# Perceiver block, fp32, one core: expert steps begun with the last feed-forward block, last expert units cut by token tile, and two reorderings in layer 1

## The reference, cut to what matters

```python
# layer 0 feed-forward: dense part plus experts chosen by product keys
mlp = silu(h @ Wg + bg) * (h @ Wu + bu) @ Wd + bd          # hidden width 2048
idx, scores = top-8 of the 64 sums of two top-8 key lists  # for each of 4 heads
w = silu(einsum('btd,bthkd->bthk', h, down_embed[idx])) * softmax(scores)
experts = einsum('bthk,bthkd->btd', w, up_embed[idx])      # 2048 experts
# layer 1 cross attention: 257 context rows of each sequence are memory keys and values
mem = ctx @ Wm; k = concat(xn @ Wk, mem); v = concat(xn @ Wv, mem)
# layer 1 MLP, both weights rounded to -1, 0, 1 times a scale of each row
tern = clip(round(w / scale), -1, 1); r = relu(x @ (tern_fc * s).T + low_rank); y = (r*r) @ (tern_proj * s).T
```

## Time and profile before

| what | us |
|---|---|
| median of 3 runs | 2406.06 (2401.96 to 2407.88) |
| the profiled execution's own time | 2407.21 |
| its span | 2405.4 |
| PE matmul busy | 2177.9 (91%) |
| DVE busy | 1260.4 (52%) |
| ACT busy | 897.4 (37%) |
| POOL busy | 92.1 (4%) |

### The profile page before, as it was taken

The page is one execution under the profiler, slowest core; times in us unless marked ns, Lnnn a source line. Parts: engine busy times, 40 slices in busy tenths (PEclk is TensorE's granted clock), DMA queues, the critical chain, the costliest instruction groups (busy, mean ns, idle before and its releaser), DMA issues. The chain is left out here.

```text
span 2405.4 us, 35121 instructions
## 1 busy us (share of the span) xinstructions
PE 2177.9 (91%) x14614; PEld 1527.3 (63%) x14614; DVE 1260.4 (52%) x2059; ACT 897.4 (37%) x2189; POOL 92.1 (4%) x113
## 2 busy tenths in 40 slices
PE   6988888779999999988998899999999999988889
PEld 4344344448876888743443688777877878764577
DVE  2103677745343877879998411244444353537553
ACT  1013333214333333369998223233232232323333
POOL 0000000000000000100000000000000000000022
PEclk9999988889999999989999889999999999999899
DMA  6010000002210011110002114421212121232000
GB/s 222 0 60 18 0 1 1 2 35 71 70 28 31 25 47 53 53 70 18 18 1 70 53 53 157 140 80 50 71 41 80 41 80 41 63 112 80 1 1 36
DMA packets 86482, 124.81 MB, mean 52 GB/s; under 512 B 7010, under 2 KB 48482, under 8 KB 86244
## 3 DMA queue, kind: packets, MB, share of 16 engines
q1 hardware_dynamic: 86324, 122.56, 15.7%
HBM read 107.60 MB, written 14.94 MB: 51 GB/s over the span
## 5 line engine op out<-in xcount | busy, mean ns | idle before, releaser
L1098 ACT ACTIVATE R<-bank 128x512 f32<-128x512 f32 (+1 forms) x155 | 91.8, 598 | 514.6 <-PE bank L808 336.6
L1339 ACT ACTIVATE R<-R 128x64 f32<-128x64 f32 x1024 | 248.8, 384 | 13.1 <-DVE R L1872 13.1
L808 PE MATMUL bank<-cth,wmh 128*128 128x512 f32 x512 | 209.2, 409 | 11.5 <-ACT arena L1403 5.5
L808 PE MATMUL bank<-cth,wml 128*128 128x512 f32 x512 | 203.3, 397 | 0.0
L808 PE MATMUL bank<-ctl,wmh 128*128 128x512 f32 x512 | 203.1, 397 | 0.0
L478 PE MATMUL bank<-H,arena 128*128 128x512 f32 x320 | 146.5, 612 | 1.5 <-ACT H L1159 0.8
L478 PE MATMUL bank<-XN,arena 128*128 128x512 f32 x320 | 146.8, 613 | 0.4 <-ACT R L1239 0.4
L478 PE MATMUL bank<-Y,arena 128*128 128x512 f32 x256 | 119.4, 613 | 6.1 <-ACT H L1345 6.1
L808 PEld LDWEIGHTS bank<-cth,wmh 128*128 128x128 f32 x512 | 96.9, 189 | 40.7 <-issue 21.2
L808 PEld LDWEIGHTS bank<-cth,wml 128*128 128x128 f32 x512 | 96.8, 189 | 22.4
L1976 DVE COPY Y<-bank 128x512 f32<-128x512 f32 x128 | 79.4, 683 | 59.4 <-PE bank L836 59.3
(11 more groups left out here) (377 smaller groups left out, 4314.4 us busy)
## 6 DMA issues: line engine op xcount, KB each, us to landing
H<-in_ctxT SPq DMA_DIRECT2D x30, 512.0 KB, 5.2
arena<-in_L_attn_mlp_w SPq DMA_DIRECT2D x8, 1024.0 KB, 5.4
arena<-spill SPq DMA_DIRECT2D x32, 256.0 KB, 5.6
spill<-R SPq DMA_DIRECT2D x3, 2048.0 KB, 8.3
spill<-XN SPq DMA_DIRECT2D x3, 2048.0 KB, 8.3
arena<-in_L_ffn_Wg SPq DMA_DIRECT2D x4, 1024.0 KB, 7.0
arena<-in_L_ffn_Wu SPq DMA_DIRECT2D x4, 1024.0 KB, 5.2
arena<-in_L_ffn_Wd SPq DMA_DIRECT2D x4, 1024.0 KB, 5.4
```

The lines of the kernel that those rows point to most:

```text
L808: last = mm(b[:, :].rearrange("p (a c) -> p a c", a=2), w_, c_[:, k, :, :], start=(k == 0 and n_ == 0), stop=(k == 3 and n_ == 2))
L1098: fn(dst, src, ACT.Copy).then_inc(act_bank_free, 1)
L1339: last = fn(EE[:, n % 2, a:a + 64], RC["Ey"][:, t, h, :], ACT.Copy, scale=RC["Ex"][:, t, h, 8 * j + x:8 * j + x + 1])
```

## The change: what it does

In the expert phase: ACT's first product is placed inside the last dense block, and waits for the routing of its own tile alone; a third product buffer is added (the space of `RC["s"]`), so that ACT may be three steps ahead of DVE's multiplication. DVE's routing pieces of tile 7 come one addition earlier, and its first `spread` comes before the last two additions of the dense part. POOL's sum waits for the last `hid_low` and is cut into eight instructions. The last four `cf` units are one token tile by 512 outputs each (16 matmuls of 128 columns) rather than one output group by 512 tokens, and the lag of PE and DVE shrinks over the last three steps. In layer 1: the memory units and feature transposes are interleaved, and key row 256 is computed as 24 matmuls with the 32 last context rows stationary and 512 columns of `Wm` moving (two units `mrow`), and turned by eight transposes within the first projection group. The `vT` split moves forward; block 4 is rounded in the last stage; blocks 4 and 5 are rounded between the additions of j = 0, blocks 6 and 7 between those of j = 1; the units `rs` 2 and 3 are computed between `f_down(j, 0)` and `f_down(j, 1)`.

```diff
+        EE = [RC["sim"][:, 0:4].rearrange("p t n -> p (t n)"), RC["sim"][:, 4:8].rearrange("p t n -> p (t n)"),
+              RC["s"].rearrange("p t n -> p (t n)")]
...
# PE, expert phase
-            for n in range(-LEAD, STEPS + LAG):
...
+            def factors_out(n):
...
+                if n >= STEPS - 4:
+                    for o in range(4):
+                        last = linear(b[:, tl(o)], W(("cf", j)), tl(o), SJ[j % 3], tl(t))
+                    last.then_inc(dve_bank_full, 1)
+                else:
                     linear(b[:, :], W(("cf", j)), tl(t % 4), SJ[j % 3], ch(t // 4)).then_inc(dve_bank_full, 1)
...
+            for n in range(LEAD):
+                factors_in(n)
+            for n in range(STEPS):
+                if n + LEAD < STEPS:
+                    factors_in(n + LEAD)
+                else:
+                    factors_out(2 * n - STEPS - 2)
+                factor_rows(n)
+                if n + LEAD >= STEPS:
+                    factors_out(2 * n - STEPS - 1)
+                elif n >= LAG:
+                    factors_out(n - LAG)
+            factors_out(STEPS - 2)
+            factors_out(STEPS - 1)
# PE, start of the cross attention
-            memory(0, range(2, 8))
-            for c in range(C2):
-                features(3, c)
+            memory(0, range(2, 5))
+            features(3, 0)
+            memory(0, range(5, 7))
+            features(3, 1)
+            memory(0, range(7, 8))
             pe.wait_ge(S["d_llo"], 1)
-            b = open_act("m256")
-            for o in range(OT1):
+            for h in range(2):
+                b = open_act(("mrow", h))
                 for k in range(4):
-                    wh, wl = wmh[:, o // 4, k, tl(o % 4)], wml[:, o // 4, k, tl(o % 4)]
-                    for i, (w_, c_) in enumerate(((wh, last_high), (wh, last_low), (wl, last_high))):
-                        last = mm(b[:, 32 * o:32 * o + 32], w_, c_[:, k, :], start=(k == 0 and i == 0), stop=(k == 3 and i == 2))
+                    for i, (c_, w_) in enumerate(((last_high, wmh), (last_low, wmh), (last_high, wml))):
+                        last = mm(b[0:32, :], c_[:, k, :], w_[:, h, k, :], start=(k == 0 and i == 0), stop=(k == 3 and i == 2))
...
# PE, last stage
-            scale_row(2, 8)
-            scale_row(3, 12)
...
                 f_down(j, 0)
+                if j < 2:
+                    scale_row(j + 2, 8 + 4 * j)
                 f_down(j, 1)
# ACT
+            def products(n):
+                j, t = n // TT, n % TT
+                if n < TT:
+                    act.wait_ge(S["c_fac"], n + 1)
+                if n >= 3:
+                    act.wait_ge(S["c_mul"], n - 2)
...
+                if j == NQ - 1:
+                    products(0)
                 exponentials_of(2 * j + 1)
...
-            act.wait_ge(S["c_fac"], TT)
-            for n in range(2):
-                products(n)
+            products(1)
+            act.wait_ge(S["h_low"], 32 + 8 * NQ)
+            products(2)
             act.wait_ge(dve_bank_full, UV.at[("cd", 3, C2 - 1, 3)] + 1)
-            hidden(0, 0)
-            products(2)
-            for t in range(1, 4):
+            for t in range(4):
                 hidden(0, t)
             products(3)
...
             f_up(0, 0)
+            f_up(0, 1)
+            ternary(4)
+            f_up(1, 0)
             ternary(5)
-            f_up(0, 1)
+            f_up(1, 1)
             ternary(6)
-            f_up(1, 0)
             ternary(7)
-            f_up(1, 1)
# DVE
+            LAST_PIECES = {(0, 0): 1, (0, 1): 2, (0, 2): 3, (0, 3): 4, (1, 0): 5}
...
+                        if (j, c, o) == (NQ - 1, 1, 1):
+                            spread(0, 0)
...
-            rounded(4, proj_row)
-            dve.wait_ge(S["f_vhi"], 1)
...
+            for j in range(NQ):
                 f_low(j, 0)
                 f_low(j, 1)
                 f_add(j, 0)
+                if j == 0:
+                    rounded(4, proj_row)
+                    rounded_up(5, 2)
+                elif j == 1:
+                    rounded_up(6, 3)
+                    rounded(7, proj_row)
                 f_add(j, 1)
# POOL
+            pool.wait_ge(S["h_low"], 32 + 8 * NQ)
             for c in range(C2):
-                g.tensor_tensor(Y[:, :, ch(c)], y_high[:, :, ch(c)].bitcast(f32), y_low[:, :, ch(c)].bitcast(f32), ALU.add
-                                ).then_inc(S["c_y"], 1)
+                for k in range(4):
+                    g.tensor_tensor(Y[:, k, ch(c)], y_high[:, k, ch(c)].bitcast(f32), y_low[:, k, ch(c)].bitcast(f32), ALU.add
+                                    ).then_inc(S["c_y"], 1)
```

More of the change, by code:

```diff
@@ new lines, in factors_in, with factor_rows @@
+            def factors_in(n):
+                j, t = n // TT, n % TT
+                if t == 0:
+                    weight(("ce", j))
+                b = open_act(("ce", j, t))
+                linear(b[:, :], W(("ce", j)), tl(t % 4), Y, ch(t // 4)).then_inc(act_bank_full, 1)
+                if t == TT - 1:
+                    free_after_act(("ce", j))
+            def factor_rows(n):
+                j, t = n // TT, n % TT
+                pe.wait_ge(S["c_p"], n + 1)
+                b = open_dve(("pt", j, t))
+                for e in range(4):
+                    last = nc.tensor.transpose(b[:, tl(e)], RC["pj"][:, t % 2, tl(e)], tab("ident"))
+                last.then_inc(dve_bank_full, 1)
@@ L810, in memory, with last_memory @@
                     last.then_inc(dve_bank_full if o in (2, 3) else act_bank_full, 1)
+            def last_memory():
+                on_act(("mrow", 1))
+                b = open_act("m256")
+                for o in range(OT1):
+                    last = nc.tensor.transpose(b[:, 32 * o:32 * o + 32], last_rows[0:32, tl(o)], tab("ident", 32)[:, 0:32])
+                last.then_inc(act_bank_full, 1)
             def projections():
@@ L1296, in _ @@
                 copy_out(RC["sim"][:, t, :], unit(("sim", t))[:, :])
+            def products(n):
+                j, t = n // TT, n % TT
+                if n < TT:
+                    act.wait_ge(S["c_fac"], n + 1)
+                if n >= 3:
+                    act.wait_ge(S["c_mul"], n - 2)
+                for h in range(PH):
+                    for x in range(8):
+                        a = 512 * h + 64 * x
+                        last = fn(EE[n % 3][:, a:a + 64], RC["Ey"][:, t, h, :], ACT.Copy,
+                                  scale=RC["Ex"][:, t, h, 8 * j + x:8 * j + x + 1])
+                last.then_inc(S["c_ee"], 1)
             def exponentials_of(t):
@@ L1329, in _ @@
                     split_high(piece_no[(("cd", j), o)] + PIECES)
-            def products(n):
-                j, t = n // TT, n % TT
-                if n >= 2:
-                    act.wait_ge(S["c_mul"], n - 1)
-                for h in range(PH):
-                    for x in range(8):
-                        a = 512 * h + 64 * x
-                        last = fn(EE[:, n % 2, a:a + 64], RC["Ey"][:, t, h, :], ACT.Copy,
-                                  scale=RC["Ex"][:, t, h, 8 * j + x:8 * j + x + 1])
-                last.then_inc(S["c_ee"], 1)
             def hidden(j, t):
@@ L1417, in _ @@
                 d_piece_high(n)
-            memory(0, (0, 1, 4, 5, 6, 7))
-            for c in range(C2):
+            memory(0, (0, 1, 4))
+            for c, more in ((0, (5, 6)), (1, (7,))):
                 features(3, c)
@@ L1422, in _ @@
                 fn(dx_high[:, :, ch(c)], XN[:, :, ch(c)], ACT.Copy).then_inc(S["d_xhi"], 1)
-            copy_out(RDm["m256"], unit("m256")[:, 0:256].rearrange("p (o b) -> p o b", o=8))
+                memory(0, more)
+            for h in range(2):
+                copy_out(last_rows[0:32, ch(h)], unit(("mrow", h))[0:32, :])
             for g_, (w, half) in enumerate(GROUPS):
@@ L1484, in _ @@
             fn(RE["z"][:, 0, :], RE["z"][:, 1, :], ACT.Exp).then_inc(S["e_exp"], 1)
-            for n in range(2, 5):
-                ternary(n)
             act.wait_ge(in_small, 112)
             fn(v_parts[:, 0], vT, ACT.Copy).then_inc(S["f_vhi"], 1)
+            for n in range(2, 4):
+                ternary(n)
             end_stage()
@@ new lines, in _ @@
+            for n in range(1, STEPS + 1):
+                if n < STEPS:
+                    spread(n // TT, n % TT)
+                if n + LEAD > STEPS:
+                    from_factors(2 * n - STEPS - 4)
+                weigh((n - 1) // TT, (n - 1) % TT)
+                if n + LEAD > STEPS:
+                    from_factors(2 * n - STEPS - 3)
+                elif n > LAG:
+                    from_factors(n - 1 - LAG)
+            dve.wait_ge(S["d_lhi"], 1)
+            v.tensor_tensor(last_low[:, :, :], last_raw, last_high[:, :, :].bitcast(f32), ALU.subtract).then_inc(S["d_llo"], 1)
@@ L2160, in _ @@
             low_rank()
-            f_low(0, 0)
-            rounded_up(5, 2)
-            f_low(0, 1)
```

(6 more changed lines are left out.)

133 lines of the change are left out of this document (64 added, 69 removed).

## The result

The changed kernel took 2338.5 us (median of 4 runs, 2331.7 to 2341.4) against 2405.9 for the kernel before (4 runs, 2402.0 to 2407.9). The ratio is 0.9719, 95% interval 0.9701 to 0.9737. The forecast was 2341, inside a range of 2332 to 2358. The profiled run took 2340.6 (span 2338.8), 66.6 less than the profiled run before; the four parts were to give 65.5.

The account below looks back on a forecast made before the run. PE was taken as the bound outside the expert phase, ACT as its pace inside. Terms of -20.7, -11.0, -17.5 and -16.3 sum to -65.5, from 2407.2 to 2341.7, given as 2341 us; range 2332 to 2358.

Parts of the forecast that it names:

- Part 1: Start of the expert phase: earlier products and POOL's sum behind `h_low` start `products(3)` near 1050.3 instead of 1070.96, -20.7 us.
- the 3 us for DVE beside POOL: Start of the expert phase: DVE loses 3 us to collisions with POOL's sum, bounds 0 and 7.
- about 7 ahead of ACT: Expert phase: at 7.7 us a step DVE reaches the last step at 1283, about 7 us ahead of ACT.
- The two rules that I weighed: DVE instructions with two SBUF inputs and POOL's SBUF reads exclude each other; those with at most one SBUF input pass.
- Part 2: Tail of the expert phase: three `cf` units by token tile instead of six cut 24.6 us to 13.6, -11.0.
- Part 3: Key row 256 in layer 1: 24 matmuls replace 96 of 32 columns and the idle time goes, -17.5 us.
- Part 4: End of layer 1, barrier and last stage: rounding and `vT` split moved, ring stall mostly removed, -16.3 us.
- The stall of 0.9: Last stage: PE wants the bank of `rs` 2 at 30.5, free at 31.4, so it stalls 0.9 us.
- A: Expert phase: DVE becomes the bound, with 7 us of POOL collisions and 7.9 a step; +7, 2349 us; 20%.
- B: Tail's three units and `mrow` units: short matmuls run at the lower clock; +11.5 + 5.4, 2358 us; 12%.
- C: Last stage: the stall only moves and the whole 10.6 us comes back; 2352 us; 10%.
- D: Expert phase falls to 1.2 GHz, 6.8 us more a step; all steps at that level give 2525 us; 3%.

Follow-up runs that it names:

- the kernel with equally slow copies: Changed kernel with key row 256 again as 96 matmuls with 32 columns moving, at its new place; 2357.3 us.
- The key row alone: Kernel before with only the key-row change (memory and feature order, last keys stationary); 2389.9 us, ratio 0.9937.
- the kernel with late products: Changed kernel with all ACT products again after the last tile is routed, three buffers kept; 2353.9 us.

## Why the prediction was right, and where its steps were off

**Part 1, forecast -20.7.** `products(3)` began 21.5 earlier, 20.4 without the 1.0 that the kernel was ahead already. Both halves were shown by undoing them (14.8 and 6.07). Of the working, the 3 us for DVE beside POOL were 4.2 and cost nothing. The margin of "about 7 ahead of ACT" at the last step was misread: it compares the start of DVE's step with the end of the phase's last `spread`. DVE began that step at 1283.15, as forecast, but ACT's last copies were ready at 1284.50 and DVE's multiplication began 0.96 us after that, so no margin was left. What I had not seen either is how near PE is at the start of the phase: with `products(3)` moved ahead, ACT waits as long for later `ce` units, so that an even earlier start brings nothing. The two rules that I weighed agree with the runs in this: an instruction with two SBUF inputs waits (9.37 us for two of 0.68), an addition from PSUM passes. But the Trainium skill (SBUF — State Buffer, section Who interferes with whom) lets an instruction with one SBUF input pass only outside the modes that use two ports, and says that a cast can enter such a mode. No trace shows the mode, but the cast L1855, with one input, took 1.08 us beside POOL for 0.18.

**Part 2, forecast -11.0.** From the end of ACT's products to layer 1 it was 29.49 us and is 18.57: -10.9. (ACT was busy without a break to 1311 only, not to 1335; behind that PE had the tail to itself but for DVE's additions and splits.) The three units took 10.96 (forecast 11.5), at the full clock. Undone, it cost 11.0 beside the kernel with equally slow copies.

**Part 3, forecast -17.5.** Measured -17.4 in the whole (-15.9 and -1.45), -18.5 alone (-17.0 and -1.45). The sum was right in its terms: the row in 5.5, no idle time, eight transposes in 0.7 (forecast 1.0), and a full-speed start of the projections worth 2.15 (forecast 2.0). That the size met so well is partly luck, since the clock of this stretch varies from run to run. The old instructions ahead of the first projection took 61.2, 56.4 and 57.9 us in three kernels, the new ones 41.0 to 45.3 in ten. In the kernel before the row's clock fell early, which made the row 1.8 longer than in the other two; in the kernel after 21 memory matmuls ran at the lower clock (until 1325.5 behind the restart at 1319.86, for one), against 14 before. Compared at the same state of the clock, part 3 is worth 16.8. The forecast took the whole 19.9 us away without saying whether the gap or the form had lowered the clock. It was the form, so the new form takes the cause away too.

**Part 4, forecast -16.3.** Measured -14.7, in three terms: the barrier -4.3 (forecast -5.8), the start of the last stage -2.9 (-2.8), the rest -7.5 (-7.7). The gap at the barrier did shrink by 5.81 (6.70 to 0.89). 1.5 of it seems lost because the pair of transposes at the stage's start took 3.68 and 3.03 us instead of 2.81 and 1.91. The key row alone, which has the old rounding, shows 3.68 there as well, and the stage took 78.85 in it; against that the change gives -5.9. And in the kernel with late products these transposes took 2.81 again, and the stage 71.44: -5.8 against before. So this is no cost of the change. The stall of 0.9 was 0.85, for the reason given: it went when the ring unit was read first.

**The rivals.** A (DVE becomes the bound): DVE waited for ACT 22 times, 8.3 us in all, in the phase; only at the end, in a step with an extra addition, was it about 1 us behind. B (short matmuls at the lower clock): the tail and `mrow` ran at 1.00, and took 10.96 and 5.5 us in every kernel that has them. The Trainium skill (TensorE: Matmul & The Clock Gate, Part 4: PE-mode transpose) says that transposes don't count as activity in the way matmuls do. No run here shows the clock falling behind the short transposes ahead of these two places. The rival's own observation, that PE can be full and stay at 1.2 GHz with 32 columns moving, was the true one, and the change removes just that. C (the stall only moves): 0.85 remained. D (the phase at 1.2 GHz): from 1050 to 1300 it was granted 0.99. The clock did fall for short times early in the phase, between PE's waits of 2.4 and 3.0 us: 0.86 and 0.83 in the windows 1060 to 1070 and 1070 to 1080.

**What the total hides.** The sum of 65.5 met 66.6, but 3.2 of these are scatter (-1.0 and -2.15), and the parts gave 63.4. Parts 1 and 2 together missed by 0.3, part 3 by 0.1, part 4 by 1.6; part 3's hit and part 4's miss both hang on the clock of a few transposes and matmuls, which differs from run to run.

## What to carry to other kernels

When an engine waits at the start of a phase, look first whether the engine that it waits for was idle at all: if not, no reordering of its list helps. If it was, follow its in-order list: a unit that needs nothing slow can stand behind one that does, and then the slow engine's pace arrives by that road. A sum on an idle engine isn't free when it reads the memory that a busy one reads too: where it started was worth 6.07 us here, how it was cut 0.6 at most. And look at which operand of a small product moves: 24 matmuls with 512 columns moving took 5.5 us where 96 with 32 columns took 18 to 20. At the 0.11 us apart of their full-speed start the 96 would take 10.6 (an estimate), so more than half of the difference is the clock.

## What the runs showed that I had not expected

- The clock fell during a run of matmuls with 32 columns moving, with PE busy all the time and no gap ahead: 0.98, then 0.50 in three windows. In the tail, with 128 columns moving (three units in 10.96 us), it did not.
- The stretch of projections and pairs has the same instructions in all kernels but for the eight transposes, and took from 758.0 to 771.7 us in fourteen profiled runs. In windows of 50 us the granted clock is 1.00 but for one or two in each: 0.93 and 0.97 where it took 771.7, 0.97 twice where it took 761.8, 0.97 once where it took 758.0. That is 0.10, 0.06 and 0.03 of 50 us, so 5, 3 and 1.5 us of PE time, and explains 2 of the 9.9 us between the first two; 1.5 is the old key row's. Another part is idle time of PE behind the projections: 26.6, 22.9 and 20.8 us in these three. Why it differs stays open; no experiment was made on it. It is large enough to hide one of the smaller parts of this change in a single run, so stretches were compared and not totals.
- A DVE cast with one SBUF input was delayed beside POOL (1.08 and 1.91 us for 0.18), and two-input instructions lost more beside longer POOL instructions: 1.55 us beside pieces of 1.3, 4.88 beside pieces of 4.6, for 0.42 alone.
- The expert phase takes as long as ACT's 1024 copies allow, and these took from 247.6 to 250.0 us in fourteen profiled runs of the same instructions.
